# Rebuilding the prologue of a TDNN, attention and mixture-of-experts kernel on one Trainium2 core

## What is computed

```python
# 1. tokens: 5 frames side by side, linear, relu, batch norm over all 3872 tokens
patches = stack of x[:, k:k+121] for k in range(5), reshaped to (32, 121, 115)
y = relu(patches @ W.T + b)
h = (y - mean(y)) * rsqrt(var(y) + 1e-5) * gamma + beta            # (32, 121, 128)
# 2. attention, 8 heads of 16; each key column has a bias per head
eb = edge_attr @ eb_w.T + eb_b                                     # 8192 edges
last[n] = the last edge with target n and both ends in 0..120, or -1
col_bias[n] = eb[last[n]] if last[n] >= 0 else 0
x1 = layernorm(h); q, k, v = linear(x1)
h = h + (softmax(q k / 4 + col_bias) v) @ o_w.T + o_b
# 3. top-1 mixture of 8 experts, 128 -> 512 -> 128, on layernorm(h)
h = h + gate * (relu(x2 @ W1[e] + b1[e]) @ W2[e] + b2[e])          # gate is 1 for top-1
```

## Time and profile before

| | us |
|---|---|
| median of 3 runs | 290.17 (289.54 to 295.07) |
| the profiled execution, time | 290.13 |
| its span, first to last instruction | 288.4 |
| PE busy / DVE / ACT / POOL | 238.1 / 184.9 / 164.8 / 141.7 |
| mean granted TensorE clock | 0.949 of full speed |

### The profile page before, as it was taken

One profiled execution on the slowest core, in us unless ns is written; L12 is line 12 of the kernel. 1 busy time (PEld: TensorE's weight loads), 2 busy tenths in 40 slices (PEclk: granted clock), 3 DMA queues, 4 the chain that ended last, 5 costly groups with the idle time before them and its releaser, 6 DMA issues.

```text
span 288.4 us, 8982 instructions
## 1 busy us (share of the span) xinstructions
PE 238.1 (83%) x2843; PEld 202.6 (70%) x2843; DVE 184.9 (64%) x716; ACT 164.8 (57%) x395; POOL 141.7 (49%) x259
## 2 busy tenths in 40 slices
PE   2899369899989899898998987875678899999960
PEld 2758157667768677686776776564568799999950
DVE  2977243476787877878778798656654465566630
ACT  2961132566676766666765655744451677777720
POOL 8001532214546657667575852425775454455550
PEclk9996567999999999999999999999997999999996
DMA  4200199200000101101101011531222553242100
GB/s 112 56 20 2 12 337 298 88 3 2 2 1 20 37 20 37 39 21 37 28 27 38 20 37 40 146 94 36 72 80 66 157 136 108 79 113 68 33 3 0
DMA packets 14461, 18.20 MB, mean 63 GB/s; under 512 B 3991, under 2 KB 10555, under 8 KB 14416
## 3 DMA queue, kind: packets, MB, share of 16 engines
q1 hardware_dynamic: 10976, 11.23, 14.3%
q0 software_dynamic: 3296, 6.00, 7.1%
q10 hardware_dynamic: 144, 0.41, 0.5%
HBM read 10.58 MB, written 7.54 MB: 63 GB/s over the span
## 4 chain that ended last, share of the span: by engine, by line
PE 59%; DVE 15%; issue 11%; ACT 4%; POOL 4%; DMA 1%; DVEq 1%; SPq 0%; ACTq 0%; POOLq 0%
PE psS L1141 9%; PE psB L1044 8%; PE psS L1060 6%; PE psU L1128 4%; PE psO L1128 4%; PE psS L1070 4%; DVE kT L725 3%; DVE nmax L861 2%; PE psB L1128 2%; PE psB L1050 2%; PE psU L1214 2%; PE psB L1033 2%; PE psO L1189 2%; PE psO L1231 2%; ACT patT L459 2%
## 5 line engine op out<-in xcount | busy, mean ns | idle before, releaser
L417 POOL DMA_INDIRECT out<-y_out,sidx x38 | 37.0, 974 | 32.6 <-DVE y_out L827 28.0
L861 DVE TENSOR_REDUCE nmax<-psS 121x8 f32<-121x968 f32 x32 | 37.3, 1165 | 17.5 <-PE psS L1070 15.6
L835 DVE TENSOR_SCALAR hT<-psS,b1T 128x128 f32<-128x128 f32 x76 | 23.3, 347 | 31.7 <-PE psS L1141 29.0
L1141 PE MATMUL psS<-xgT,W_tile 128*128 128x128 f32 x304 | 40.9, 278 | 0.0
L410 POOL DMA_INDIRECT region_d<-rows,pos x32 | 34.7, 1085 | 9.2 <-issue 8.9
L570 ACT ACTIVATE PT<-psS 121x968 f32<-121x968 f32 x32 | 31.3, 978 | 13.3 <-DVE nmax L861 11.0
L1141 PEld LDWEIGHTS psS<-xgT,W_tile 128*128 128x128 f32 x304 | 37.8, 195 | 0.0
L526 ACT ACTIVATE hT<-psS,b1T 128x128 f32<-128x128 f32 x76 | 23.7, 363 | 13.3 <-PE psS L1141 13.2
L1060 PE MATMUL psS<-kT,qT 32*121 32x121 f32 x512 | 22.5, 289 | 8.9 <-DVE kT L725 6.5
L1060 PEld LDWEIGHTS psS<-kT,qT 32*121 32x121 f32 x512 | 17.0, 180 | 16.8 <-issue 9.8
L507 ACT ACTIVATE W_tile<-W_sb 128x512 f32 x38 | 23.9, 630 | 6.6 <-issue 3.7
(11 more groups left out here) (250 smaller groups left out, 580.4 us busy)
## 6 DMA issues: line engine op xcount, KB each, us to landing
xg<-region_d SPq DMA_DIRECT2D x38, 129.0 KB, 2.1
W_sb<-in_L_ffn_W SPq DMA_DIRECT2D x1, 2048.0 KB, 9.5
region_d<-pads SPq DMA_DIRECT2D x1, 1032.0 KB, 6.7
out<-y_out,sidx POOLq DMA_INDIRECT x38, 2.3
b_bc<-in_L_ffn_b SPq DMA_DIRECT2D x1, 512.0 KB, 5.1
region_d<-rows,pos POOLq DMA_INDIRECT x32, 3.0
xs<-in_x ACTq DMA_DIRECT2D x1, 402.5 KB, 3.6
edge_i<-in_L_attn_edge_index SPq DMA_DIRECT2D x1, 64.0 KB, 4.0
```

What stands on the lines that cost most here:

```text
L417: pool.indirect_dma_start(out, bass.IndirectOffsetOnAxis(sidx[:, s:s + 1], 0), y_out[:, u, :], None, bounds_check=N - 1, oob_is_err=False) ...
L861: dve.tensor_reduce(nmax[0:L, :].rearrange("p (j c) -> p j c", c=HB)[:, :, HD + 1:HD + 3], score_half(0), AX.X, ALU.max, negate=True).then ...
L1141: ins = pe.matmul(psS[:, c // 2 * 2 + s % 2, c % 2 * 128:(c % 2 + 1) * 128], W1_tile[:, s % 2, c * 128:(c + 1) * 128], xgT[:, s % 2, :], s ...
```

## The change

- POOL makes the identity first (new semaphore `s_ident`); `s_const` now counts 18.
- PE begins with two patch groups, then the token weights, a third group, the key, and so on; patch groups sit in the banks of `PATCH_BANK`, the edge bits in bank 2, the transposed weights in bank 1.
- The one-hots are 64 comparisons with a per-partition scalar (keyT is f32 now), all ahead of the first bn_stats. The tiny matmuls are split: 32 ahead of the y matmuls, 32 behind them.
- ACT copies the q, k, v weights and Wr after its relus, the bias columns after the first batch_norm, and squares pair 0. DVE's `owX` copy stands behind the column search.
- The q and k bias products stand behind the second half of the tiny matmuls; h0 of pairs 0 and 1 ahead of the o-weight and bias matmuls.
- The transposes of h0 of pair 2 stand behind the projections of pair 0, those of xn of pair 1 in step 0 (both through psO); the step loop waits only for xT of pair 0. The squares of pair 2 move into step 0.

```diff
-        keyT = sb("keyT", [128, EF], BF16)
+        keyT = sb("keyT", [128, EF])
...
-        N_CONST = 20
+        N_CONST = 18
+        PATCH_BANK = (3, 4, 5, 6, 7, 0, 3, 4)
...
+            pool.memset(ident[:, :], 0.0).then_inc(s_ident, 1)
+            pool.wait_ge(s_ident, 1)
+            pool.affine_select(out=ident[:, :], in_=ident[:, :], compare_op=ALU.not_equal, fill=1.0, base=0,
+                               pattern=[[-1, 128]], channel_multiplier=1).then_inc(s_ident, 1)
             pool.memset(qk_row[:, :, :], 0.0).then_inc(s_rowset, 1)
...
-            pool.memset(ident[:, :], 0.0).then_inc(s_const, 1)
...
-            pool.wait_ge(s_const, 18)
-            pool.affine_select(out=ident[:, :], in_=ident[:, :], compare_op=ALU.not_equal, fill=1.0, base=0,
-                               pattern=[[-1, 128]], channel_multiplier=1).then_inc(s_const, 1)
+            pool.wait_ge(s_const, 17)
...
+            act.wait_ge(a_w4, 1)
+            for n, w in enumerate((qwT, kwT)):
+                act.activation(w[:, :].rearrange("p (h c) -> p h c", c=HB)[:, :, 0:HD],
+                               banks[1][:, n * D:(n + 1) * D].rearrange("p (h c) -> p h c", c=HD),
+                               ACT.Identity).then_inc(a_wts, 1)
+            act.activation(vwT[:, :], banks[1][:, 2 * D:3 * D], ACT.Identity).then_inc(a_wts, 1)
+            act.wait_ge(a_wrc, 1)
+            act.activation(idX[:, 0:E], banks[1][:, 384:384 + E], ACT.Identity).then_inc(a_wts, 1)
...
             act.wait_ge(a_ac, 1)
-            act.wait_ge(a_wts, 7)
             batch_norm(0)
+            act.wait_ge(a_bias, 1)
+            act.activation(qk_col[:, 0:2], banks[5][:, 0:2], ACT.Identity, scale=0.25).then_inc(a_wts, 1)
+            act.activation(qk_col[:, 2:4], banks[5][:, 2:4], ACT.Identity).then_inc(a_wts, 1)
             h0_copy(0, banks[6])
+            act.wait_ge(s_h0k, 1)
+            for k in range(2):
+                act.activation(sq1[0:L, k, :], h0k[0:L, 0, k, E:E + D], ACT.Square, accum_out=ss1[0:L, k:k + 1]).then_inc(s_sq1, 1)
             batch_norm(1)
-            xT_copy(0, banks[1])
             h0_copy(1, banks[7])
             batch_norm(2)
+            xT_copy(0, banks[1])
+            act.wait_ge(a_wts, 7)
             q_copy(0, banks[7])
-            h0_copy(2, banks[0])
+            h0_copy(2, psO)
             batch_norm(3)
-            xT_copy(1, banks[3])
 
             for t in range(STEPS):
                 p, even = t // 2, t % 2 == 0
+                if t == 0:
+                    xT_copy(1, psO)
...
+            dve.wait_ge(s_ident, 2)
+            dve.tensor_scalar(idX[:, E:E + D], ident[:, :], -1.0 / D, None, ALU.add).then_inc(a_cen, 1)
             dve.wait_ge(l_edges, 16)
-            dve.wait_ge(s_const, N_CONST)
-
-            dve.tensor_scalar(idX[:, E:E + D], ident[:, :], -1.0 / D, None, ALU.add).then_inc(a_cen, 1)
...
-            link(dve.tensor_copy(keyT[:, :], banks[0][:, 128:128 + EF]))
+            dve.tensor_copy(keyT[:, :], banks[0][:, 128:128 + EF]).then_inc(a_keyT, 1)
             dve.tensor_copy(tokWT[0:CTX * DI, :], banks[0][0:CTX * DI, 0:128]).then_inc(a_wts, 1)
-
-            def target_onehots(c):
-
-                dve.tensor_tensor(target1h[:, 8 * c:8 * c + 8, :],
-                                  slot_iota[:, 1:L + 1].unsqueeze(1).to_broadcast([128, 8, L]),
-                                  keyT[:, 8 * c:8 * c + 8].unsqueeze(2).to_broadcast([128, 8, L]),
-                                  ALU.is_equal).then_inc(a_1h, 1)
-
-            target_onehots(0)
-            target_onehots(1)
...
-            dve.wait_ge(a_w4, 1)
-            for n, w in enumerate((qwT, kwT)):
-                dve.tensor_copy(w[:, :].rearrange("p (h c) -> p h c", c=HB)[:, :, 0:HD],
-                                banks[1][:, n * D:(n + 1) * D].rearrange("p (h c) -> p h c", c=HD)).then_inc(a_wts, 1)
-            dve.tensor_copy(vwT[:, :], banks[1][:, 2 * D:3 * D]).then_inc(a_wts, 1)
-            target_onehots(2)
-            dve.wait_ge(a_bias, 1)
-            dve.wait_ge(a_wrc, 1)
-            dve.tensor_scalar(qk_col[:, 0:2], banks[2][:, 0:2], 0.25, None, ALU.mult).then_inc(a_wts, 1)
-            dve.tensor_copy(qk_col[:, 2:4], banks[2][:, 2:4]).then_inc(a_wts, 1)
-            dve.tensor_copy(idX[:, 0:E], banks[2][:, 8:8 + E]).then_inc(a_wts, 1)
-            target_onehots(3)
-            target_onehots(4)
+            dve.wait_ge(a_keyT, 2)
+
+            for c in range(8):
+                for f in range(8 * c, 8 * c + 8):
+                    ins = dve.tensor_scalar(target1h[:, f, :], slot_iota[:, 1:L + 1], keyT[:, f:f + 1], None, ALU.is_equal)
+                ins.then_inc(a_1h, 1)
             for c in range(NCH):
                 dve.wait_ge(a_relu, c + 1)
                 dve.bn_stats(bn_st[:, c, :], yT[:, c * CH:(c + 1) * CH]).then_inc(a_bst, 1)
-                if c % 2 == 1 and c < 7:
-                    target_onehots(5 + c // 2)
             dve.wait_ge(a_bst, NCH)
             dve.bn_aggr(bn_mv[:, :], bn_st[:, :, :].rearrange("p a b -> p (a b)")).then_inc(a_var, 1)
...
-            dve.wait_ge(a_owp, 1)
-            dve.tensor_copy(owX[:, :], banks[4][:, 0:WX]).then_inc(a_owx, 1)
...
             dve.wait_ge(a_rstd, 1)
...
-            bits = banks[3][0:L, 0:EF * EG]
-            dve.wait_ge(a_bits, 1)
+            bits = banks[2][0:L, 0:EF * EG]
+            dve.wait_ge(a_bits, 8)
...
             dve.tensor_scalar(last_i[0:L, :], last[0:L, 0:1], -127.0 - 128 // EG, 0.0, ALU.add, ALU.max).then_inc(a_lasti, 1)
+            dve.wait_ge(a_owp, 1)
+            dve.tensor_copy(owX[:, :], banks[4][:, 0:WX]).then_inc(a_owx, 1)
...
+            squares1(1)
...
-            squares1(0)
-            squares1(1)
...
+            dve.wait_ge(a_wts, 7)
...
             k_copy(0)
-            squares1(2)
...
-                if even and p >= 1 and p + 2 < NP:
+                if even and p + 2 < NP:
                     squares1(p + 2)
...
-            pe.wait_ge(s_const, N_CONST)
+            def patches(t):
+
+                if t == 5:
+                    pe.wait_ge(a_wts, 1)
+                if t > 5:
+                    pe.wait_ge(a_pat, t - 5)
+                for i in range(4 * t, min(4 * t + 4, SEG + 1)):
+                    ins = pe.transpose(banks[PATCH_BANK[t]][0:CTX * DI, (i - 4 * t) * 128:(i - 4 * t + 1) * 128],
+                                       xs[:, i * DI:(i + CTX) * DI], ident[:, :])
+                ins.then_inc(a_xt, 1)
+
+            def edge_bits(c):
+
+                pe.wait_ge(a_1h, c + 1)
+                for f in range(8 * c, 8 * c + 8):
+                    ins = pe.matmul(banks[2][0:L, f * EG:(f + 1) * EG], target1h[:, f, :], power_bf[:, :], start=True, stop=True)
+                ins.then_inc(a_bits, 1)
+
+            pe.wait_ge(s_ident, 2)
+            pe.wait_ge(l_x, 16)
+            patches(0)
+            patches(1)
             pe.wait_ge(l_tokW, 16)
             pe.transpose(banks[0][0:CTX * DI, 0:128], tokW_sb[:, :], ident[:, :]).then_inc(a_wt, 1)
...
-            for t in range(8):
-                if t == 2:
-                    pe.wait_ge(a_keyed, 1)
-                    pe.transpose(banks[0][:, 128:128 + EF], key[:, :], ident[0:EF, 0:EF]).then_inc(a_keyT, 1)
-                if t == 5:
-                    pe.wait_ge(l_proj, 64)
-                    for n in range(3):
-                        ins = pe.transpose(banks[1][:, n * D:(n + 1) * D], proj_in[:, n, :],
-                                           ident[:, :])
-                    ins.then_inc(a_w4, 1)
-                if t == 6:
-                    pe.wait_ge(l_qkb, 32)
-                    for n in range(4):
-                        ins = pe.matmul(banks[2][:, n:n + 1], qk_row[0:1, n // 2, n % 2 * 128:n % 2 * 128 + 128],
-                                        ident[0:1, 0:1], start=True, stop=True)
-                    ins.then_inc(a_bias, 1)
-                    pe.wait_ge(a_cen, 1)
-                    pe.wait_ge(l_wr, 16)
-                    pe.matmul(banks[2][:, 8:8 + E], idX[:, E:E + D], Wr_sb[:, :], start=True, stop=True).then_inc(a_wrc, 1)
-                if t >= 5:
-                    pe.wait_ge(a_wts, (1, 4, 7)[t - 5])
-                bank = banks[(3 + t) % 8]
-                for i in range(4 * t, min(4 * t + 4, SEG + 1)):
-                    ins = pe.transpose(bank[0:CTX * DI, (i - 4 * t) * 128:(i - 4 * t + 1) * 128],
-                                       xs[:, i * DI:(i + CTX) * DI], ident[:, :])
-                ins.then_inc(a_xt, 1)
+            patches(2)
+            pe.wait_ge(a_keyed, 1)
+            pe.transpose(banks[0][:, 128:128 + EF], key[:, :], ident[0:EF, 0:EF]).then_inc(a_keyT, 1)
+            patches(3)
+            patches(4)
+            pe.wait_ge(l_proj, 64)
+            for n in range(3):
+                ins = pe.transpose(banks[1][:, n * D:(n + 1) * D], proj_in[:, n, :], ident[:, :])
+            ins.then_inc(a_w4, 1)
+            for t in range(5, 8):
```

(52 more changed lines are left out.)

8 lines of the change are left out of this document (4 added, 4 removed).

## The result

| | before | after |
|---|---|---|
| median of 4 runs each, us | 290.06 (289.54 to 295.07) | 285.73 (285.12 to 286.42) |
| the profiled execution, time | 290.13 | 285.12 |
| its span | 288.4 | 283.3 |
| first scores | 43.46 | 39.62 |
| second row maximum | 49.00 | 43.94 |

A forecast was written before the change was run, and what follows sets the result against it. The prologue's chain of waits, not PE's throughput, was taken as the bound. Column search 3.5 us earlier, first scores 6.4; after step 0, 6.3 was taken between 5.7 and 7.1: 290.13 - 6.3 = 283.8 us, range 281.8 to 286.8.

The forecast's parts named there:

- line at 2%: Whole kernel: 5.8 us faster, at 284.4 us, as the least difference told from no change; faster given 0.58.
- the outcome that had 0.38: Whole kernel: the verdict "same", a difference under 2%, chance 0.38.
- y's start to the last relu's end: Prologue, PE and ACT: stays 7.46 us as before, so the last relu ends at 21.05.
- slack of PE before xn's transpose: PE's new order ahead of xn's transpose: its chain ends at 31.2, 0.15 us before xn is ready.
- xn ready to first scores: Stretch from xn to first scores: 8.62 - 2.09 - 1.48 + 0.55 = 5.6 us.
- the statistics term: One-hots, bn_stats and owX ahead of the column search: search begins at 23.8 instead of 27.31, gain 3.5 us.
- wrong above 0.18: DVE's 64 one-hot comparisons: prediction wrong if their pitch exceeds 0.18 us each; 0.14 was taken.
- 0.3 us that I gave for cheaper ones: Statistics, if 16-bit comparisons are cheaper by the skill's rule: paced by ACT alone, 0.3 us earlier.
- the rival that I gave 0.17: Clock falls under y, with 32 tiny matmuls before it: half speed for 3.4 us, loses 1.7, 285.5 us; chance 0.17.
- clock low anywhere from 13 to 20: Prologue around y: a stated sign that the prediction is wrong.
- a late order on PE: Rival: squares near their upper bound or x landing 0.7 later; 1.4 us of gain lost, 285.2 us; chance 0.17.
- step 0, put at -0.1: Step 0 after first scores: total gain 5.7 us with clock as before, 7.1 with it high; 6.3 taken between.

The follow-up runs named there:

- short chain: Eight wide comparisons, weight copies before relus, o-weight matmul right behind y, owX and bias matmuls earlier, pair 0's norm off POOL's gather queue, against the changed kernel: 289.45 us, ratio 0.9735.
- the run with a constant: Changed kernel with its 64 comparisons against a constant instead of the key column (does not compute the layer): 291.69 us, one execution.
- the run with the clock held: Changed kernel's comparisons, all tiny matmuls behind y, three unused 484-column matmuls filling PE's gap before y: 291.57 us, one execution.
- scores waiting: Changed kernel with the first scores waiting again for pair 1's transposes and pair 2's squares: 295.75 us, one execution.
- 128 wide: Changed kernel with each comparison over all 128 slots, aligned, instead of 121: 285.41 us, one execution.
- eight wide comparisons ahead: Changed kernel with its 64 comparisons put back to eight tensor_tensor ones of 968 elements, all ahead of the statistics: 283.54 us, ratio 0.9754.
- both together: Changed kernel with eight tensor_tensor comparisons ahead of the statistics and all 64 tiny matmuls behind y: 285.46 us, ratio 0.9807.
- the filled version with wide comparisons: The "both together" kernel plus three unused f32 matmuls of 484 columns in PE's gap before y: 292.66 us, ratio 0.9856.
- group A: Runs on one chip with the kernel before beside them, before measuring 290.62 us.
- B and C: Two further groups of runs, each on one chip beside the kernel before: 297.22 us in B, 298.08 us in C.

## Why the prediction was right, and where it was not

The mechanism held: the same chain, shortened ahead of the second maximum, and the rest carried along unchanged (239.4 us in both). The 1.4% falls short of the line at 2% to which I gave 0.58; it is the outcome that had 0.38. By its steps, in the profiled executions:

| step | predicted gain or time | measured |
|---|---|---|
| first patch copy | 5.77 | 5.84 |
| y starts | 13.6 | 14.14 |
| comparison | 0.14, one-hots end 17.3 | 0.161, 18.67 |
| y's start to the last relu's end | 7.46 | 9.1 |
| last bn_stats ends | 21.95 | 23.97 |
| from there to the search | 1.85 | 1.84 |
| column search | 23.8 (gain 3.5) | 25.81 (gain 1.5) |
| search to xn ready | 7.53 | 7.53 |
| squares on ACT, a pair | 0.75 | 0.70 (28.37 to 29.07) |
| slack of PE before xn's transpose | 0.15 | 0.38 |
| xn ready to first scores | 5.6 | 6.28 |
| first scores | 37.0 (gain 6.4) | 39.62 (gain 3.84) |
| gain at the second maximum | 6.3 | 5.06 |

**The step that was mis-sized is the statistics term, 3.5 us, which measured 1.5.** Two causes, and the runs set them in a square of column-search times:

| | clock high under y | clock low under y |
|---|---|---|
| eight wide comparisons | 23.94, 23.98, 23.70 | 25.13 |
| 64 comparisons with a column | 25.18 | 25.81, 25.67, 25.87, 26.00 |

(The low and wide one is the short chain, whose other edits leave the 1.85 us between bn_stats and search as they were; the run with a constant, quick comparisons and the clock low, gives 25.02 beside it. 23.98 and 23.70 hold a wait of 0.25 to 0.27 for the tiny matmuls.) Either alone costs 1.1 to 1.5 us; together they cost some 2.0, since bn_stats end at the later of two paces, DVE's and y's.

*The comparisons:* I took 0.14 from a row of another operation with an immediate scalar, and said that I would be wrong above 0.18. But what mattered was not that bound: at 0.161 the chain is already late by 64 x 0.021 = 1.3 us, because DVE has no slack there (the run with the clock held measured 25.18 - 23.8 = 1.4). Of the Trainium skill ("VectorE: DVE Perf Modes", the section on the perf-mode tiers) I wrote that by its rule these comparisons would be cheaper than the f32 one. Its table is for 2048 elements, these have 121. They were dearer: 121 bf16 elements took 0.161 us with the column, 0.10 with a constant, and one tensor_tensor did the work of eight of them in 1.08 us against 1.29. (The 0.3 us that I gave for cheaper ones is 0.2 by my own two ends, 21.95 and 21.75.)

*The clock:* the rival that I gave 0.17 happened, at the place named and for the time named (low from 14.5 to 17.9, 3.4 us), but the tiny matmuls that I named with it are not needed: the clock fell in a run with none ahead of y, and in one with all in a row. With quick comparisons its price was 1.1 to 1.4 us, near my 1.7. On top of the slow comparisons the low column lies only 0.5 to 0.8 behind the high one, and even that is not the clock's alone: there y also started at 14.0 to 14.3, held by the comparisons, and not at 13.30. With all tiny matmuls behind y, y started at 13.65, and the clock fell under it; but bn_stats kept DVE's own pace (4.60 us), and without its 0.64 of waiting for the tiny matmuls the search would have stood at 25.45, 0.27 behind the 25.18, of which 0.2 is a later start of DVE. So this rival came true and still does not decide: with slow comparisons the low clock by itself cost next to nothing in that one profile, and the 0.5 to 0.8 needs their hold on y's start as well.

**What offset it.** From the search to the second maximum I expected a gain of 2.8 (6.3 less 3.5), and it was 3.56 (18.13 against 21.69). The freed scores give 1.7 of that (the run that takes it back). The path from xn to the scores was 0.7 worse than said: both projections took 3.56 at the low clock, not 3.2, and small gaps of 0.15 before and 0.2 behind them were not counted. Step 0 was better: from the scores to the second maximum 4.32 against 5.54, 1.2 us gained, where I had taken a loss of 0.1 as a mean between the clock high (+0.7) and low. The clock was back at 1.00 from 39 on, somewhat later than the 37 I gave, and was 1.00 over step 0 (40 to 48), where it had been 0.66 from 43 to 48; no run sets the clock's part in the 1.2 us apart.

The condition "clock low anywhere from 13 to 20" was met, and by it alone I would have called myself wrong. The range held partly by luck. Its upper end took the clock's loss together with a late order on PE; PE was not late (0.38 of slack), and in that place stood a loss that I had not summed, the comparisons' 1.3 us at a pitch inside the bound of 0.18. And step 0, put at -0.1, gave 1.2 back. The median of 285.73 lies 1.9 above the forecast: 1.3 us is this sum, 0.6 the difference between the profiled execution and the median.

**What stays open.** What brings the clock down under y. With PE's gap filled it stayed high in all three profiles. Unfilled, it fell in seven profiles of the changed order (the changed kernel twice, tiny matmuls behind y, 128 wide, constant, scores waiting, short chain) and stayed in two (eight wide comparisons ahead, both together). The six of these with 64 separate comparisons all fell, of the three with wide ones only the short chain; no run tells whether that is chance. Before it stayed high too, with PE only 0.26 busy from 13 to 14:

```profile
13.00:14.00 1.00, 0.26 (x3) 0.06 (x1) 1.00 (x2) 1.00 (x2) 0.00 (x0) 1.00 0.63 207
14.00:15.00 1.00, 0.51 (x2) 0.30 (x2) 0.77 (x1) 0.44 (x2) 0.00 (x0) 1.00 0.78 320
```

In "both together" PE even stood idle for 2.62 us ahead of y and the clock stayed; with 2.76 us, in the run with the tiny matmuls behind y, it fell. So an idle stretch of this kind does not suffice to bring it down, and three profiles do not prove that filling prevents it. The Trainium skill ("TensorE: Matmul & The Clock Gate", "Why this matters for your kernels") names idle gaps as the cause. Filling agrees with that; the changed kernel, whose longest gap ahead of the fall was 0.68 us, and the fall of before between 23 and 24, with PE 1.00 busy, do not. It also stays open why the filled version with wide comparisons, 1.6 us earlier at the second maximum than the changed kernel, shows the same ratio (0.9856 against 0.986; both intervals are 1.1 us or more to each side). What lies behind the second maximum varies by more than that: 239.4 us in the first profiles of both kernels, 239.4 to 242.4 in group A, 246.3 to 248.3 in B and C (247.4 for the changed kernel once more). That it was equal to 0.1 us before and after is therefore a property of that pair, and the whole time of a single execution ranks no prologue.
